# A two-layer attention kernel: minima first on VectorE, fewer reads of PSUM on ScalarE, and Q and K two slots earlier in steps without an MLP

## The reference, cut to what matters

```python
tgt1 = _layer_norm(tgt, g1, be1)
tgt = tgt + _self_attn(tgt1, mask, ...)        # pass 0, with an arbitrary additive mask
tgt = tgt + (memory @ Wg.T + bg)
ff = jax.nn.relu(_layer_norm(tgt, g2, be2) @ W1.T + b1) @ W2.T + b2
...
x = x + mha(ln1(x), ln1(x), causal=True)       # pass 1, causal self-attention, no MLP behind it
x = x + mha(ln2(x), encoded, causal=False)     # pass 2, attention over the context
x = x + relu(ln3(x) @ w1 + b1) @ w2 + b2
```

## Time and profile before

| | |
|---|---|
| median of 3 runs | 1724.61 us (1707.62 to 1731.74) |
| the profiled execution | 1704.09 us, span 1702.3 us |
| busy, share of the span | PE 86%, DVE 71%, ACT 62%, POOL 49% |
| chain that ended last | PE 42%, issue 13%, ACT 12%, DVE 12%, DMA 9%, POOL 6% |
| granted TensorE clock, mean | 0.956 |

### The profile page before, as it was taken

How to read it: one execution, slowest core, us unless ns; L and a number is a source line. 1 busy time by engine, 2 the same in 40 slices (tenths; PEclk the granted TensorE clock), 3 DMA queues, 4 the chain that set the end, 5 groups by cost and what they waited for, 6 DMA issues and landing times.

```text
span 1702.3 us, 42833 instructions
## 1 busy us (share of the span) xinstructions
PE 1459.5 (86%) x13376; PEld 1175.9 (69%) x13376; DVE 1212.1 (71%) x3855; ACT 1061.9 (62%) x2153; POOL 834.7 (49%) x1125
## 2 busy tenths in 40 slices
PE   2789999999998998878787777778999999999986
PEld 1567788877777887765566555555777777777756
DVE  2688887888878887656666766666776777677742
ACT  3677676777777775445565555556656665666552
POOL 3345454444444566544344443444555655565533
PEclk8799999999999999989899999998999999999989
DMA  5645555444544455444655646574644364546300
GB/s 145 139 113 119 108 109 118 99 99 105 117 100 99 105 125 130 119 107 107 124 121 111 129 101 140 115 153 93 119 112 105 99 128 99 105 101 129 79 26 13
DMA packets 163511, 185.75 MB, mean 109 GB/s; under 512 B 15952, under 2 KB 140240, under 8 KB 163408
## 3 DMA queue, kind: packets, MB, share of 16 engines
q1 hardware_dynamic: 163408, 184.57, 49.8%
HBM read 125.78 MB, written 58.72 MB: 108 GB/s over the span
## 4 chain that ended last, share of the span: by engine, by line
PE 42%; issue 13%; ACT 12%; DVE 12%; DMA 9%; POOL 6%; SPq 5%; ACTq 1%; DVEq 0%; POOLq 0%
PE d_ps L437 16%; PE d_ps L673 8%; DMA k_stack<-parts 7%; PE o_ps L572 5%; PE s_ps L494 5%; PE t_ps L542 3%; DVE prob L858 3%; PE t_ps L508 3%; SPq L399 2%; DMA parts<-q_part 2%; ACT prob_t L721 2%; SPq L404 2%; DVE o_n L890 2%; POOL h_lo L1031 2%; PE m_ps L444 1%
## 5 line engine op out<-in xcount | busy, mean ns | idle before, releaser
L721 ACT ACTIVATE prob_t<-t_ps 128x384 f32<-128x384 f32 (+1 forms) x512 | 275.4, 551 | 393.0 <-PE t_ps L542 197.7
L494 PE MATMUL s_ps<-k_stack,q_stack 96*128 96x256 bf16 (+1 forms) x1536 | 294.6, 275 | 124.5 <-DMA k_stack<-parts 47.5
L712 ACT ACTIVATE prob<-prob,neg_max 128x256 f32<-128x256 f32 x512 | 233.8, 514 | 121.0 <-DVE neg_max L858 118.8
L494 PEld LDWEIGHTS s_ps<-k_stack,q_stack 96*128 96x128 bf16 x1536 | 115.1, 100 | 227.8 <-issue 65.7
L542 PE MATMUL t_ps<-q_stack,k_stack 108*128 108x256 bf16 (+1 forms) x1024 | 207.3, 269 | 23.0 <-ACT prob_t L721 14.3
L858 DVE CUSTOM_DVE_ANT_0 prob<-s_ps,bias_sb 128x256 f32<-128x256 f32 x512 | 192.4, 416 | 48.5 <-PE s_ps L494 36.7
L858 DVE CUSTOM_DVE_ANT_0 prob<-s_ps,causal 128x128 f32<-128x128 f32 (+1 forms) x512 | 158.5, 352 | 90.2 <-PE s_ps L494 88.0
L843 DVE TENSOR_REDUCE top<-s_ps 128x2 f32<-128x512 f32 x256 | 172.9, 682 | 54.8 <-PE s_ps L494 51.3
L1031 POOL TENSOR_TENSOR h_lo<-h_f,h_hi 128x512 fp32r<-128x512 f32 x128 | 165.9, 1296 | 86.6 <-DVE h_hi L921 86.6
L572 PE MATMUL o_ps<-prob_t,v_sb 128*17 128x256 f32 (+1 forms) x3072 | 200.7, 381 | 0.0
L437 PE MATMUL d_ps<-x2t_hi,w_hi 128*128 128x256 f32 x512 | 157.0, 307 | 38.2 <-ACT k_f L780 21.8
(11 more groups left out here) (115 smaller groups left out, 4063.5 us busy)
## 6 DMA issues: line engine op xcount, KB each, us to landing
q_stack<-parts SPq DMA_DIRECT2D x288, 128.0 KB, 4.0
k_stack<-parts SPq DMA_DIRECT2D x288, 128.0 KB, 6.4
parts<-q_part SPq DMA_DIRECT2D x96, 192.0 KB, 2.3
parts<-k_part SPq DMA_DIRECT2D x96, 192.0 KB, 2.3
ct_kept<-ct_hl SPq DMA_DIRECT2D x16, 512.0 KB, 8.0
x_in<-x_mid SPq DMA_DIRECT2D x32, 256.0 KB, 2.9
x_res<-x_mid SPq DMA_DIRECT2D x32, 256.0 KB, 3.0
ct_hl<-ct_kept SPq DMA_DIRECT2D x16, 512.0 KB, 8.2
```

The costliest lines, as they stand in the source:

```text
L494: last = mm(s_ps[:, h % 2, q * S:q * S + n], q_stack[0:ROWS, t.par, HEAD[h], q * P:(q + 1) * P], k_stack[0:ROWS, t.par, HEAD[h], 0:n], sta ...
L712: last = nc.scalar.activation(prob[:, h % 4, q, :], prob[:, h % 4, q, :], ACT.Exp, bias=neg_max[:, h % 4, q:q + 1], scale=-1.0)
L721: nc.scalar.activation(prob_t[:, h % 8, 0:n], t_ps[:, h % 2, 0:n], ACT.Exp, scale=-1.0)\
```

## The change

1. On DVE the minimum and the odd copy stand first in a slot, not last. The statistics, mean and normalisation of `st.nxt2` move from slots 9, 10 and 12 to 4, 5 and 6; normalising the output in pass 0 moves from slots 6 and 7 to 7 and 8. The sum with epsilon moves to POOL. V of passes 1 and 2 is copied by ACT, not by DVE.
2. ACT reads each PSUM bank once, into float32 (with two instructions of 256 where a bias goes by column, else with one of 512), and makes the first part from SBUF with one more instruction, `high_part`, which waits for the float32 to be there. POOL's subtraction now waits for that.
3. In steps without an MLP in `st.old`, Q and K stand in slots 0 and 1, not 2 and 3, and their split and stacking follow two slots earlier on ACT, POOL, DVE and SP (`qk_at`).
4. The matmuls that turn the minima over write 108 rows (96 of them zero) with the whole array, not 12 rows with a tile position. The causal mask is kept once.

```diff
-NORM_AT = (6, 10, 10)
+NORM_AT = (7, 10, 10)
+STATS_AT, MEAN_AT, HAT_AT = 4, 5, 6
...
+        eps_sb = sb("eps_sb", [P, NPASS, TT])
...
-        top_part = sb("top_part", [P, 2, TT, CH, NSPLIT], BF16)
+        top_wide = sb("top_wide", [P, 2, TT, ROWS + TOP], BF16)
...
+
+        def qk_at(st):
+
+            return 2 if has(st.old, MLP) else 0
...
-                if h == 6 and has(st.nxt):
+                if h == qk_at(st) + 4 and has(st.nxt):
...
-                if h == 7 and has(st.nxt):
+                if h == qk_at(st) + 5 and has(st.nxt):
...
-                    last = mm(o_ps[ROWS:ROWS + TOP, S + q * P:S + (q + 1) * P],
-                              top_part[:, c % 2, q].rearrange("p j n -> p (j n)"), ident_bf[:, :],
-                              start=True, stop=True, tile_position=(0, ROWS))
+                    last = mm(o_ps[0:ROWS + TOP, S + q * P:S + (q + 1) * P], top_wide[:, c % 2, q, :], ident_bf[:, :],
+                              start=True, stop=True)
...
-                if h == 2 and has(st.nxt):
+                if h == qk_at(st) and has(st.nxt):
                     weights(st.nxt, UNIT_QKV)
-                    pe.wait_ge(xt_f.sem, xt_f.after(st.nxt))
+                    pe.wait_ge(xt_h.sem, xt_h.after(st.nxt))
...
-                if h == 3 and has(st.nxt):
+                if h == qk_at(st) + 1 and has(st.nxt):
...
-            def affine(high, dst, col_g, col_b, done):
-
-                for out_t in (high, dst):
-                    for k in range(KC):
-                        last = nc.scalar.activation(out_t[:, k, :], m_ps[:, k * S:(k + 1) * S], ACT.Identity,
-                                                    bias=cols_sb[:, col_b + k:col_b + k + 1],
-                                                    scale=cols_sb[:, col_g + k:col_g + k + 1])
+            def affine(dst, col_g, col_b, done):
+
+                for k in range(KC):
+                    last = nc.scalar.activation(dst[:, k, :], m_ps[:, k * S:(k + 1) * S], ACT.Identity,
+                                                bias=cols_sb[:, col_b + k:col_b + k + 1],
+                                                scale=cols_sb[:, col_g + k:col_g + k + 1])
                 last.then_inc(done.sem, 1)
+
+            def high_part(task, dst, src, made, done):
+
+                act.wait_ge(made.sem, made.after(task))
+                act.sem_inc(passed, 1)
+                nc.scalar.activation(dst, src, ACT.Copy).then_inc(done.sem, 1)
...
-                    affine(x2t_hi, tf_b, c, c + 2, x2t_f)
-                if h == 3 and has(st.nxt):
+                    affine(tf_b, c, c + 2, x2t_f)
+                    high_part(st.old, x2t_hi[:, :, :], tf_b[:, :, :], x2t_f, x2t_h)
+                if h == qk_at(st) + 1 and has(st.nxt):
                     act.wait_ge(q_mm.sem, q_mm.after(st.nxt))
                     if st.cur:
                         act.wait_ge(q_p3.sem, q_p3.after(st.cur))
+                    if st.nxt.p == 0:
...
+                    else:
+                        last = nc.scalar.activation(q_f[:, :, :], d_ps[:, 1, :].rearrange("p (m s) -> p m s", m=KC),
+                                                    ACT.Copy, scale=-0.25)
+                    last.then_inc(q_done.sem, 1)
+                    if st.cur:
                         act.wait_ge(q_written.of(st.cur), q_written.after(st.cur))
-                    act.sem_inc(passed, 1)
...
-                    last.then_inc(q_done.sem, 1)
-                if h == 4 and has(st.nxt):
+                    high_part(st.nxt, q_part[:, 0], q_f[:, :, :], q_done, q_p1)
+                if h == qk_at(st) + 2 and has(st.nxt):
...
+                        last = nc.scalar.activation(k_f[:, :, :], d_ps[:, 0, :].rearrange("p (m s) -> p m s", m=KC),
+                                                    ACT.Copy)
+                    last.then_inc(k_done.sem, 1)
+                    if st.cur:
                         act.wait_ge(k_written.of(st.cur), k_written.after(st.cur))
...
-                                                        ACT.Copy)
-                    last.then_inc(k_done.sem, 1)
+                    high_part(st.nxt, k_part[:, 0], k_f[:, :, :], k_done, k_p1)
...
+                    nc.scalar.activation(tf_b[:, :, :], m_ps[:, :].rearrange("p (k s) -> p k s", k=KC), ACT.Copy)\
+                        .then_inc(ct_f.sem, 1)
+                    if st.old:
                         act.wait_ge(proj_mm.sem, proj_mm.after(st.old))
                         act.wait_ge(ct_stored.of(st.old), ct_stored.after(st.old))
-                    turned = m_ps[:, :].rearrange("p (k s) -> p k s", k=KC)
-                    act.sem_inc(passed, 1)
-                    nc.scalar.activation(ct_hi[:, :, :], turned, ACT.Copy)
-                    nc.scalar.activation(tf_b[:, :, :], turned, ACT.Copy).then_inc(ct_f.sem, 1)
+                    high_part(st.prev, ct_hi[:, :, :], tf_b[:, :, :], ct_f, ct_h)
...
+                if h == V_AT + 1 and has(st.nxt, KEYED):
+                    act.wait_ge(v_mm.sem, v_mm.after(st.nxt))
+                    if st.prev:
+                        act.wait_ge(pv_mm.sem, pv_mm.after(st.prev))
+                    act.sem_inc(passed, 1)
+                    nc.scalar.activation(v_sb[:, st.nxt.par, :, :, 0:HD],
+                                         d_ps[:, 1, :].rearrange("p (k h d) -> p k h d", k=TT, d=HD), ACT.Copy)\
+                        .then_inc(v_done.sem, 1)
...
-                    affine(xt_hi, tf_a, c, c + 2, xt_f)
+                    high_part(st.nxt2, xt_hi[:, :, :], tf_a[:, :, :], xt_f, xt_h)
...
                     last = v.bn_aggr(mv_t[:, t, :], st_t[:, t, :])
                 last.then_inc(mv_done.sem, 1)
-                dve.wait_ge(mv_done.sem, mv_done.after(task))
-                v.tensor_scalar(ve_t[:, :], mv_t[:, :, 1], eps, None, ALU.add).then_inc(ve_done.sem, 1)
...
             def slot(st, h):
+                if has(st.cur):
+                    score_guard(st, h)
+                t, ht = head_at(st, h, LAG, (0,))
+                if t and ht % 2:
+                    dve.wait_ge(t_mm.sem, t_mm.after(t, ht + 1))
+                    ring_free(dve, st, t, ht)
+                    v.tensor_copy(prob_t[:, ht % 8], t_ps[:, 1, :]).then_inc(pt_odd.sem, 1)
...
-                if h == 5 and has(st.nxt):
+                if h == qk_at(st) + 3 and has(st.nxt):
...
-                if h == 6 and has(st.nxt):
+                if h == qk_at(st) + 4 and has(st.nxt):
...
-                if h == 9 and has(st.nxt2):
+                if h == STATS_AT and has(st.nxt2):
...
-                if h == 10 and has(st.nxt2):
+                if h == MEAN_AT and has(st.nxt2):
...
-                    aggregate(st.nxt2, stats, mv, ve, LN_EPS[st.nxt2.p], ln_stats, ln_mv, ln_ve)
-                if h == V_AT + 1 and has(st.nxt):
...
+                if h == V_AT + 1 and has(st.nxt, (0,)):
...
-                            last = v.tensor_tensor(dst, src, bv, ALU.add)
-                        else:
-                            last = v.tensor_copy(dst, src)
+                        bv = rows_sb[:, R_BV, :].rearrange("p (h d) -> p h d", d=HD)
+                        last = v.tensor_tensor(dst, src, bv, ALU.add)
                     last.then_inc(v_done.sem, 1)
-                if h == 12 and has(st.nxt2):
+                if h == HAT_AT and has(st.nxt2):
...
-                if has(st.cur):
-                    score_guard(st, h)
...
-                if h == 4 and has(st.nxt):
-                    pool.wait_ge(q_done.sem, q_done.after(st.nxt))
+                if h == qk_at(st) + 2 and has(st.nxt):
+                    pool.wait_ge(q_p1.sem, q_p1.after(st.nxt))
...
-                    pool.wait_ge(k_done.sem, k_done.after(st.nxt))
+                if h == qk_at(st) + 3 and has(st.nxt):
+                    pool.wait_ge(k_p1.sem, k_p1.after(st.nxt))
...
-                if h == 6 and has(st.nxt):
+                if h == qk_at(st) + 4 and has(st.nxt):
...
-                if h == 10 and has(st.nxt2):
+                if h == MEAN_AT and has(st.nxt2):
+                    pool.wait_ge(ln_mv.sem, ln_mv.after(st.nxt2))
+                    pool.sem_inc(passed, 1)
+                    g.tensor_tensor(ve[:, :], mv[:, :, 1], eps_sb[:, st.nxt2.p], ALU.add).then_inc(ln_ve.sem, 1)
```

76 lines of the change are left out of this document (35 added, 41 removed).

## The result

| | before | changed |
|---|---|---|
| median | 1720.15 us (4 runs, 1707.62 to 1731.74) | 1890.74 us (4 runs, 1881.46 to 1892.98) |
| ratio | | 1.0988, 95% interval 1.0911 to 1.1065 |
| span of the profiled execution | 1702.3 us | 1879.7 us |
| granted clock, mean | 0.956 | 0.902 |
| step in passes 0, 1, 2 | 39.2, 27.6, 34.0 us | 43.8, 31.9, 36.6 us |

What follows compares the result with a forecast made beforehand. PE was busy for most of passes 0 and 2; pass 1 was bound by the loop from scores through Q, K, DRAM and stacked reads. Terms -5 +20 -3 = +12 on 1724.6 gave 1736.6 us, range 1662 to 1778.

Steps and rivals of the forecast that it cites:

- Pass 0, +20 us forecast: Pass 0, minima first: V 2.05 us later, less 0.65 saved, 1.4 us a step over 14 steps; between -2 and +39.
- The 0.65 us that I counted as saved on the minima: Pass 0: of PE's 1.0 us a step of waits for minima, 0.65 was counted as saved.
- rival (b): Pass 0's clock falls to 0.92: 3.1 us a step, +44, 1781 us; chance 0.18, shared with another new wait that size.
- The normalising at slot 6: Pass 0, DVE: normalising `x_in`, newly ahead of the second `h_hi`, counted as 2 x 0.4 us.
- Pass 1, -5 us forecast: Pass 1, Q and K two slots earlier: 0.3 us off a step over 15 steps; bounds -35 and +15.
- Pass 2, -3 us forecast: Pass 2: `k_f` wait goes, mostly lost to POOL's added work; 0.2 us a step over 14 steps, between -26 and +10.
- Rival (a): Pass 1's loop shortened in full, waits in all passes vanish: 98 us less, 1627 us; chance 0.20 for it or most.
- The rule on shared ports: Pass 0: two-input DVE and GpSimd SBUF instructions exclude each other, so `o_n` stays long, 1 us a step worse than short.

Runs made afterwards that it cites:

- e13: The kernel before with the minima first, except in slots 7 to 10 of steps with an MLP and in slots 14 and 15; 1768.06 us, ratio 1.032.
- e7: The changed kernel with DVE's order and the slots of Q and K put back, the early first norm left in; 1752.84 us, ratio 1.021.
- e4: The changed kernel with DVE's order, the slots of Q and K and those of the first norm put back; 1688.33 us, ratio 0.985.
- e9: The changed kernel with only the first norm put back, and the first normalising of o at slot 6; 1831.69 us, ratio 1.067.
- e11: e7 with the normalising of x put back from slot 6 to slot 12; 1722.45 us, ratio 1.001.
- e1: The kernel before with one edit: minima and odd copies first in each DVE slot; 1820.49 us, ratio 1.061.
- e2: The kernel before with one edit: Q and K two slots earlier in steps without an MLP; 1730.55 us, ratio 1.010.
- e12: The changed kernel with X^T also two slots earlier in steps without an MLP; 1869.11 us, ratio 1.086.
- e14: e1 with the transposes of o_q ahead of the minima again; 1794.31 us, ratio 1.046.
- e10: e4 with V copied by DVE again instead of ACT; 1687.62 us, ratio 0.980.
- e3: The kernel before with one edit: the split minima brought to PSUM by a full-width product, the causal bias held once; 1713.75 us, ratio 1.001.

## Why the prediction was wrong

The forecast was 1736.6 us, the range ended at 1778, and the measured median is 1890.7.

- **Pass 0, +20 us forecast, about +64 measured** (4.6 a step over 14). The chain was right: `h_hi`, POOL, the fourth `h_f`, V. The second `h_hi` was to end at 23.2 us of the step and ended at 23.9; the second `h_lo` was to start at 23.3, it was 24.0; V was to wait 2 to 3 us and waited 2.4; no `k_f` wait over 1 us. Some of that is luck: from slot 6's minimum on, DVE took 8.7 us where 8.8 was the middle of the sum, because `x_in` took 2.6 us and not 0.8, while `o_n`, `k_part` and the two `h_hi` all ran at the low end of their ranges. The first `h_hi` was to be 2 to 3 us later and is 3.8. The step that failed is the one from V's delay to the length of a step. The 0.65 us that I counted as saved on the minima were none (14.2 us of waits for `neg_max` against 11.6 in the window). The wait for `x_hat`, 1.0 us a step, I had at nothing; e13, with the minima last in slots 14 and 15, has none. And rival (b), to which I gave 0.18 together with any other new wait of its size, held: ten of twelve steps were below full clock, six of them at 0.92 or less, and PE's busy time grew by 2.2 us a step, as much as its waits.
- **The normalising at slot 6.** I priced it at 2 x 0.4 us from the medians of the earlier trace rows, and at nothing beside that. In its new place it takes 2.6 us for two, while POOL works on K's third part and the context. e7 against e4 and e9 against the changed kernel put 59 to 64 us on the early norm, the second largest part, and e11 puts on this instruction all of it in pass 0 and two thirds in pass 2. The longer time alone does not explain it: from e4 to e7 `x_in` grew from 20.4 to 30.4 us in pass 0, but `o_n` fell from 20.9 to 9.1, and DVE's busy time stayed (388.9 and 389.3). What it stands in front of counts: the wait for POOL's root (0.85 us in the step shown) and the block itself are now ahead of head 6's minimum and the first `h_hi`.
- **Pass 1, -5 us forecast, about +69 measured.** This is the step that failed most. That "Q's matmuls start right behind them", the scores, is false: they start 2.2 us behind. I followed Q and K forward and never asked when `xt_lo` is ready, though ACT makes the high part in slot 14 and POOL the low one in slot 15, one slot ahead of the new Q. I also wrote that the minima first would cost nothing there, because PE would wait that much longer for the stacked K. Instead `top_rows` waits for `o_q` and for the splitting (54 us together), and the stacked K, whose wait was to be as large as before or larger, is waited for 0.2 us in all. PE's waits grew by 37 us and its busy time by 34, at a clock of 0.82 for 0.92. The transfer of Q, foretold at 10 to 11 us of a step at full clock, starts at 12 to 15 us (18.6 in the first step), and no step was at full clock. e1, e2, e12 and e14 tell the parts apart.
- **Pass 2, -3 us forecast, about +37 measured** (2.6 a step over 14). The wait for `k_f` was to go and fell from 8.6 to 3.6 us. Reading PSUM once, with the epsilons on POOL, is in truth worth 1.3 to 1.4 us a step (e4, e10), more than the 0.2 that I kept. It is buried under the `o_q` waits of the minima first (e14) and the early norm (e9). The first is nowhere in my sum, and of the second only POOL's part.
- **Rival (a)** fell: the wait for the stacked K did vanish, as it had it, and pass 1 got longer all the same. **The full-width product** was rightly held to be free (e3).
- **The rule on shared ports** that I weighed on `o_n` pointed at the right mechanism and the wrong instruction. `o_n` ran at its short value in the changed kernel's pass 0 (0.42 us each on average, with POOL idle beside it in the step shown); the normalising took 1.28 to 1.38 each in all 24 cases of pass 0, against 0.40 to 0.75 before. The Trainium skill ("SBUF — State Buffer", "Who interferes with whom") counts `tensor_scalar` among the operations that can take the port pair shared with GpSimd, so the trace agrees with it there.

Left open: the last 2 us a step of e13, pass 1 of e11, what the odd copies cost apart from the minima, which every run moves together, what the epsilons on POOL give, and how much of the loss is the clock alone, since nothing was run that changes the clock and no wait.

## What to carry to other kernels

In an in-order queue, putting the job that waits for the busiest engine first makes every ready job behind it late by that wait; in no run here did it pay. Price a moved instruction by what runs beside it at its new place and by what it will stand in front of, and when you pull a consumer forward, walk back from its operands first. And where several waits of 1 to 3 us are added to an engine that was nearly always busy, count the fall of its clock as likely: by PE's busy time it cost as much as the longer waits did in passes 0 and 1 (26.9 and 34.0 us against 26.9 and 37.0), and a third as much in pass 2 (7.2 against 22.6).
